# Two mixture-of-experts layers around an attention layer: the routing worked from the logits, and the slot-index matmuls moved to a place of their own

## The reference, cut to what matters

```python
x = x + 0.5 * ffn(layernorm(x)); x = x + attn(layernorm(x)); x = x + 0.5 * ffn(layernorm(x))   # x: 2 x 1024 x 128
def ffn(hidden_states):                        # N = 2048 tokens, E = 32 experts, TOP_K = 8, CAPACITY = 128, F = 96
    logits = x @ gate_weight.T
    probs = softmax(logits); topw, topi = top_k(probs, 8); topw = topw / topw.sum(-1, keepdims=True)
    pos = (cumsum(one_hot(flat_e), axis=0) * one_hot).sum(-1) - 1      # place in the expert's queue
    buf = zeros(E, 128, 128).at[flat_e, pos].set(flat_x, mode='drop')  # only the first 128 tokens of an expert
    gate, up = split(einsum('ech,efh->ecf', buf, gate_up_proj))
    eo = einsum('ecf,ehf->ech', silu(gate) * up, down_proj)
    out = (eo.at[flat_e, pos].get(fill_value=0) * flat_w[:, None]).sum(over the 8)
```

## Time and profile before

| what | before |
|---|---|
| time, median of 3 runs | 618.35 us (617.75 to 620.77) |
| the profiled execution: its own time, its span | 620.18 us, 618.5 us |
| granted clock of TensorE over the span | 0.928 |
| busy: PE, DVE, ACT, POOL | 529.7 us (86%), 431.8 (70%), 253.3 (41%), 94.9 (15%) |
| the chain that ended last | PE 69%, DVE 18%, issue 5%, ACT 4%, DMA 2% |
| DMA | 32.47 MB, mean 52 GB/s |

### The profile page before, as it was taken

How to read it: one execution, slowest core, us unless ns; L and a number is a source line. 1 busy time by engine, 2 the same in 40 slices (tenths; PEclk the granted TensorE clock), 3 DMA queues, 4 the chain that set the end, 5 groups by cost and what they waited for, 6 DMA issues and landing times.

```text
span 618.5 us, 11436 instructions
## 1 busy us (share of the span) xinstructions
PE 529.7 (86%) x3411; PEld 336.7 (54%) x3435; DVE 431.8 (70%) x1404; ACT 253.3 (41%) x405; POOL 94.9 (15%) x208
## 2 busy tenths in 40 slices
PE   2867999867798999999999999999987636899986
PEld 1745787653373555555555555555533533577764
DVE  5875888764659476777867677767810787879874
ACT  3523122123361456564555556554576320121212
POOL 3700000001500112131221212121222150000000
PEclk9679899987798799999999999999999758899999
DMA  8694221000061000000000000000020000112102
GB/s 232 176 283 138 76 77 45 32 2 3 0 258 67 1 21 26 12 25 27 27 27 26 28 16 25 15 26 27 0 80 0 1 1 0 39 47 71 49 27 69
DMA packets 27502, 32.47 MB, mean 52 GB/s; under 512 B 7009, under 2 KB 18753, under 8 KB 27329
## 3 DMA queue, kind: packets, MB, share of 16 engines
q1 hardware_dynamic: 26784, 31.61, 16.9%
q10 hardware_dynamic: 672, 0.28, 0.2%
HBM read 21.76 MB, written 9.96 MB: 51 GB/s over the span
## 4 chain that ended last, share of the span: by engine, by line
PE 69%; DVE 18%; issue 5%; ACT 4%; DMA 2%; SPq 1%; DVEq 1%; ACTq 0%; POOL 0%
PE ps L1271 12%; PE ps L1336 11%; PE ps L1061 10%; PE ps L1309 9%; PE ps L1093 7%; PE ps L1105 5%; DVE mxh L925 3%; PE ps L1112 3%; PE ps L1002 2%; DVE summed L922 2%; PE ps L1267 2%; ACT probs L663 1%; PE ps L1211 1%; PE ps L1065 1%; PE ps L1013 1%
## 5 line engine op out<-in xcount | busy, mean ns | idle before, releaser
L663 ACT ACTIVATE probs<-ps 128x1024 f32<-128x1024 f32 (+2 forms) x192 | 148.2, 810 | 128.1 <-PE ps L1309 128.0
L925 DVE TENSOR_REDUCE mxh<-ps 128x1 f32<-128x512 f32 (+2 forms) x176 | 117.5, 690 | 50.3 <-PE ps L1271 48.3
L1271 PE MATMUL ps<-Kst,Qst 120*128 120x512 f32 (+3 forms) x384 | 137.4, 422 | 7.5 <-DVE mxh L925 4.3
L1271 PEld LDWEIGHTS ps<-Kst,Qst 120*128 120x128 f32 x384 | 68.5, 196 | 66.8 <-DVE mxh L925 23.7
L1309 PE MATMUL ps<-Qst,Kst 121*128 121x512 f32 (+3 forms) x384 | 96.3, 357 | 1.9 <-ACT probs L663 1.7
L922 DVE CUSTOM_DVE_ANT_0 summed<-ps,maskf 128x384 f32<-128x384 f32 (+1 forms) x128 | 76.2, 621 | 23.1 <-PE ps L1271 21.3
L495 POOL TENSOR_SCALAR_AFFINE_SELECT probs<-probs 128x256 f32<-128x256 f32 x128 | 52.0, 406 | 232.5 <-ACT probs L663 231.8
L1336 PE MATMUL ps<-probs,Vst 128*32 128x512 f32 (+3 forms) x768 | 82.7, 503 | 1.2 <-POOL probs L495 1.2
L1309 PEld LDWEIGHTS ps<-Qst,Kst 121*128 121x128 f32 x384 | 67.5, 192 | 22.4 <-ACT probs L663 7.3
L1061 PE MATMUL ps<-onehot,xp 128*128 128x512 bf16 (+1 forms) x245 | 68.2, 397 | 9.5 <-DVE onehot L785 8.0
L785 DVE TENSOR_SCALAR onehot<-iotab,posm 128x128 bf16<-128x128 bf16 (+1 forms) x352 | 59.2, 247 | 3.3 <-issue 2.5
(11 more groups left out here) (167 smaller groups left out, 595.1 us busy)
## 6 DMA issues: line engine op xcount, KB each, us to landing
gus<-guT_d SPq DMA_DIRECT2D x14, 384.0 KB, 3.5
wgn<-in_L_ffn_gate_up_proj SPq DMA_DIRECT2D x8, 384.0 KB, 4.9
guT_d<-gus SPq DMA_DIRECT2D x8, 384.0 KB, 4.6
dns<-dnT_d SPq DMA_DIRECT2D x14, 192.0 KB, 3.4
Kst<-kn_d SPq DMA_DIRECT2D x28, 64.0 KB
Qst<-qn_d SPq DMA_DIRECT2D x28, 64.0 KB
wdn<-in_L_ffn_down_proj SPq DMA_DIRECT2D x8, 192.0 KB, 5.5
dnT_d<-dns SPq DMA_DIRECT2D x8, 192.0 KB, 5.1
```

The lines of the kernel that those rows point to most:

```text
L663: e.activation(probs[n % RING][:, 2 * b:2 * b + 2, lo:BANK], ps[:, 2 * b:2 * b + 2, lo:BANK], ACT.Exp, scale=SCALE).then_inc(probs_ready, 1)
L925: e.tensor_reduce(to, s.rearrange("p (q k) -> p q k", k=w), AX.X, ALU.max).then_inc(mx_ready, 1)
L1271: ins = e.matmul(ps[:, bank, i * w:(i + 1) * w], Qst[p][h][0:ROWS, column(b, jt * P):column(b, jt * P) + P], Kst[p][h][0:ROWS, column(b, o ...
```

## The change

- `route` reads the logits from a copy that ScalarE makes (`copy_logits`), takes the eight largest of them directly, and leaves the softmax and the weights out of the path to `posm`.
- The 15 position matmuls become one: VectorE first sums the mask over the tiles up to each tile, with four additions of shifted copies (`upto[1]` to `upto[4]`, shifts 1, 2, 4 and 8, over zeroed pads that GpSimd writes).
- The weights are made by `weigh`, on VectorE between the one-hots of chunks 0 and 1, and their three parts by GpSimd in `write_info`, after its `split`.
- The small index matmuls leave `gather` and become `find(c)`, run in step `c` after `gather(c + 1)`; the one-hots get a second buffer, and `slots(c)` runs in step `c` in the place where `slots(c + 1)` ran. ScalarE's `eoh` of `c` still waits for `slots(c)`.
- `exps(0)` follows the fourth weight copy on ScalarE instead of preceding the second.

```diff
-        maskb = sb("maskb", [P, NT, E], BF16, moe)
+        upto = [sb(f"upto{i}", [P, NT // 2 + NT, E], BF16, moe) for i in range(5)]
+        maskb = upto[0][:, NT // 2:, :]
...
-        onehot = sb("onehot", [P, NT, CE, CAP], BF16, moe)
+        onehot = [sb(f"onehot{p}", [P, NT, CE, CAP], BF16, moe) for p in range(RING)]
...
             def split(k):
+                for i in range(4):
+                    e.memset(upto[i][:, 0:NT // 2, :], 0.0).then_inc(pads, 1)
...
+            def write_info(k):
+                e.wait_ge(pr_ready, k + 1)
+                e.tensor_copy(info[:, :, :, 2], pr[:, :, :]).then_inc(info_step, 1)
+                e.wait_ge(info_step, 3 * k + 1)
+                e.tensor_tensor(wr[:, :, :], pr[:, :, :], info[:, :, :, 2], ALU.subtract).then_inc(info_step, 1)
+                e.wait_ge(info_step, 3 * k + 2)
+                e.tensor_copy(info[:, :, :, 3], wr[:, :, :]).then_inc(info_step, 1)
+                e.wait_ge(info_step, 3 * k + 3)
+                e.tensor_tensor(info[:, :, :, 4], wr[:, :, :], info[:, :, :, 3], ALU.subtract).then_inc(info_ready, 1)
             split(0)
+            write_info(0)
...
+            def copy_logits(k):
+                e.wait_ge(logits_done, k + 1)
+                e.activation(flat(wr[:, :, :]), ps[:, 2, :], ACT.Copy).then_inc(lg_copied, 1)
             def exps(k):
-                e.wait_ge(soft, 2 + 5 * k)
...
             copy_weights(0, 0)
-            exps(0)
+            copy_logits(0)
             copy_weights(1, 1)
-            with e.Fori(1, NCH // RING) as i:
-                for p in range(RING):
-                    e.wait_ge(w_stored[p], 32 * i)
-                    copy_weights(i * RING + p, p)
+            for s in range(RING, NCH):
+                e.wait_ge(w_stored[s % RING], 32 * (s // RING))
+                copy_weights(s, s % RING)
+                if s == RING + 1:
+                    exps(0)
             experts(0)
...
-                s0 = 5 * k
-                lg = ps[:, 2, :].rearrange("p (t e) -> p t e", t=NT)
...
-                e.wait_ge(logits_done, k + 1)
-                e.tensor_reduce(top[:, :], lg, AX.X, ALU.max).then_inc(soft, 1)
-                e.wait_ge(soft, s0 + 1)
-                e.tensor_tensor(zl[:, :, :], lg, wide_of(top), ALU.subtract).then_inc(soft, 1)
-                e.wait_ge(exp_done, k + 1)
-                e.tensor_reduce(den[:, :], zl[:, :, :], AX.X, ALU.add).then_inc(soft, 1)
-                e.wait_ge(soft, s0 + 3)
-                e.reciprocal(rden[:, :], den[:, :]).then_inc(soft, 1)
-                e.wait_ge(soft, s0 + 4)
-                e.tensor_tensor(pr[:, :, :], zl[:, :, :], wide_of(rden), ALU.mult).then_inc(soft, 1)
-                e.wait_ge(soft, s0 + 5)
+                e.wait_ge(lg_copied, k + 1)
                 for t in range(NT):
-                    e.max(t8[:, t, :], pr[:, t, :]).then_inc(top8, 1)
+                    e.max(t8[:, t, :], lg[:, t, :]).then_inc(top8, 1)
                 e.wait_ge(top8, NT * (k + 1))
                 for t in range(NT):
-                    e.match_replace(rep[:, t, :], t8[:, t, :], pr[:, t, :], -1.0).then_inc(replaced, 1)
+                    e.match_replace(rep[:, t, :], t8[:, t, :], lg[:, t, :], LOWEST).then_inc(replaced, 1)
                 e.wait_ge(replaced, NT * (k + 1))
-                q0 = 8 * k
-                e.tensor_scalar(maskb[:, :, :], rep[:, :, :], 0.0, None, ALU.is_lt).then_inc(routed, 1)
-                e.tensor_reduce(den[:, :], t8[:, :, :], AX.X, ALU.add).then_inc(routed, 1)
-                e.wait_ge(routed, q0 + 2)
-                e.reciprocal(rden[:, :], den[:, :]).then_inc(routed, 1)
-                e.tensor_tensor(wr[:, :, :], pr[:, :, :], maskb[:, :, :], ALU.mult).then_inc(routed, 1)
-                e.tensor_scalar(zl[:, :, :], rep[:, :, :], 0.0, UNROUTED, ALU.is_ge, ALU.mult).then_inc(posm_ready, 1)
-                e.wait_ge(routed, q0 + 4)
-                e.scalar_tensor_tensor(out=pr[:, :, :], in0=wr[:, :, :], scalar=0.25, in1=wide_of(rden), op0=ALU.mult, op1=ALU.mult).then_inc(routed, 1)
-                e.wait_ge(routed, q0 + 5)
-                e.wait_ge(info_const, 2 * (k + 1))
-                e.tensor_copy(info[:, :, :, 2], pr[:, :, :]).then_inc(routed, 1)
-                e.wait_ge(routed, q0 + 6)
-                e.tensor_tensor(wr[:, :, :], pr[:, :, :], info[:, :, :, 2], ALU.subtract).then_inc(routed, 1)
-                e.wait_ge(routed, q0 + 7)
-                e.tensor_copy(info[:, :, :, 3], wr[:, :, :]).then_inc(routed, 1)
-                e.wait_ge(routed, q0 + 8)
-                e.tensor_tensor(info[:, :, :, 4], wr[:, :, :], info[:, :, :, 3], ALU.subtract).then_inc(onehot_ready[k], 1)
+                e.tensor_scalar(maskb[:, :, :], rep[:, :, :], TAKEN, None, ALU.is_lt).then_inc(routed, 1)
+                e.wait_ge(routed, k + 1)
+                e.wait_ge(pads, 4 * (k + 1))
+                for i in range(4):
+                    src, half = upto[i], NT // 2
+                    e.tensor_tensor(upto[i + 1][:, half:, :], src[:, half:, :], src[:, half - (1 << i):half + NT - (1 << i), :], ALU.add).then_inc(summed_up, 1)
+                    if i < 3:
+                        e.wait_ge(summed_up, 4 * k + i + 1)
+                e.tensor_tensor(zl[:, :, :], lg[:, :, :], t8[:, :, 0:1].broadcast_to([P, NT, E]), ALU.subtract).then_inc(soft, 1)
+                e.tensor_scalar(rep[:, :, :], rep[:, :, :], TAKEN, UNROUTED, ALU.is_ge, ALU.mult).then_inc(posm_ready, 1)
...
+            def weigh(k):
+                e.wait_ge(exp_done, k + 1)
+                e.tensor_tensor(wr[:, :, :], zl[:, :, :], maskb[:, :, :], ALU.mult).then_inc(weigh_step, 1)
+                e.wait_ge(weigh_step, 3 * k + 1)
+                e.tensor_reduce(den[:, :], wr[:, :, :], AX.X, ALU.add).then_inc(weigh_step, 1)
+                e.wait_ge(weigh_step, 3 * k + 2)
+                e.reciprocal(rden[:, :], den[:, :]).then_inc(weigh_step, 1)
+                e.wait_ge(weigh_step, 3 * k + 3)
+                e.scalar_tensor_tensor(out=pr[:, :, :], in0=wr[:, :, :], scalar=0.25, in1=wide_of(rden), op0=ALU.mult, op1=ALU.mult).then_inc(pr_ready, 1)
...
-                    e.wait_ge(gathered, u + 1)
+                    e.wait_ge(indexed, u + 1)
...
                         place_slots(c - 1, 1 - p)
-                    if ahead >= 1:
-                        slots(c + 1, 1 - p)
+                    slots(c, p)
...
-                    if ahead >= 2:
-                        onehots(c + 2)
-                onehots(0)
-                slots(0, 0)
-                onehots(1)
+                    if ahead:
+                        onehots(c + 2, p)
+                onehots(0, 0)
+                weigh(k)
+                onehots(1, 1)
...
-                e.wait_ge(routed, 8 * k + 1)
-                e.matmul(ps[:, 3, :], zerosb[:, 0:P], zerosb[:, :], start=True, stop=False, skip_group_check=True)
-                for t in range(NT - 1):
-                    o = ps[:, 3, (t + 1) * E:].rearrange("p (t e) -> p t e", e=E)
-                    e.matmul(o, onesb[:, :], maskb[:, t:t + 1, :].broadcast_to([P, NT - 1 - t, E]),
-                             start=False, stop=False, skip_group_check=True)
-                e.matmul(ps[:, 3, :], beforeb[:, :], flat(maskb[:, :, :]), start=False, stop=True, skip_group_check=True).then_inc(pos_done, 1)
+                e.wait_ge(routed, k + 1)
+                e.matmul(ps[:, 3, :], beforeb[:, :], flat(maskb), start=True, stop=False, skip_group_check=True)
+                e.wait_ge(summed_up, 4 * (k + 1))
+                e.matmul(ps[:, 3, E:], onesb[:, :], flat(upto[4][:, NT // 2:NT // 2 + NT - 1, :]), start=False, stop=True,
+                         skip_group_check=True).then_inc(pos_done, 1)
...
                     u = k * NCH + c
                     e.wait_ge(bufT_ready, u + 1)
+                    def tile(t, first=False, last=False):
+                        e.wait_ge(onehot_ready[k], c * n + t + 1)
+                        for part in range(3):
+                            ins = e.matmul(ps[:, 0, :], xp[:, bass.ds(t, 1), part, :].rearrange("p o d -> p (o d)"),
+                                           onehot[p][:, bass.ds(t, 1), :, :].rearrange("p o e c -> p (o e c)"),
+                                           start=first and part == 0, stop=last and part == 2, skip_group_check=True)
+                        if last:
+                            ins.then_inc(gathered, 1)
...
+                def find(c, p):
...
                     e.wait_ge(idx_ready, u + 1)
+                    e.wait_ge(info_ready, k + 1)
...
-                            ins = e.matmul(ps[:, 3, q * 8:q * 8 + 5], onehot[:, bass.ds(t, 1), q, :].rearrange("p o c -> p (o c)"),
+                            ins = e.matmul(ps[:, 3, q * 8:q * 8 + 5], onehot[p][:, bass.ds(t, 1), q, :].rearrange("p o c -> p (o c)"),
```

(23 more changed lines are left out.)

30 lines of the change are left out of this document (14 added, 16 removed).

## The result

| | before | after |
|---|---|---|
| time, median | 618.68 us (617.75 to 620.77, 4 runs) | 641.99 us (634.62 to 648.47, 4 runs) |
| ratio | 1 | 1.0328, 95% interval 1.0288 to 1.0367 |
| the profiled execution, its span | 620.18, 618.5 | 634.62, 632.8 |

The change costs 3.3%, some 20 us. The ratio leaves out the run of 648.47 us, which was in a slower state that some executions show; the medians, which take it in, are 23 us apart. The prediction was 619.2, with a range up to 623.0: the time lies far above it, on the side of the third rival. The profiled execution is the fastest of the four, so the trace shows only 14.3 us of loss.

The account below looks back on a forecast made before the run. TensorE was taken to pace the middle steps, VectorE close behind; VectorE alone bounds the second routing. First layer -3.7 + 2.2 + 1.5 = 0.0, second -3.3 + 2.4 + 1.5 + 0.3 = +0.9: 619.2 us against 618.35, range 614.4 to 623.0.

Parts of the forecast that it names:

- the third rival: The series of index matmuls on TensorE isn't hidden: 628 us at the worst, 624 in the middle; chance 0.12.
- the last term of the steps: Index matmuls in one series on TensorE: the queue runs ahead under row matmuls, 0.3 us added in the second stage.
- The sign that the prediction had named: Gaps over 0.4 us in TensorE's index series would show the prediction wrong.
- late slots: Middle steps: `eoh` waits for `wslot`, now computed in the same step, so VectorE idles; +2.2 and +2.4 us per stage.
- Routing: Second layer's routing: one-hots start 6.6 us earlier, near 511.1, with four additions of 0.45 us each.
- The exclusion of GpSimd and the one-hots: Second start: GpSimd's 5.9 us and chunk 1's 4.0 us of one-hots run one after the other; gain 3.3, not 7.3.
- Rival (1): GpSimd and the one-hots don't exclude each other, so the second start keeps 7.3: 615.2 us; chance 0.17.
- First layer: First layer's start: the last weight transpose starts at 45.1, gate/up of chunk 0 at 48.2, a gain of 3.7 us.
- rival (2): The starts gain more as weight loads finish earlier, or `eoh` waits less: 2 to 4 us less, 616; chance 0.10.
- The last step: Last step of each layer: no one-hots hide the late slots, so `eol`, `place` and `combine` come later; +1.5 us.
- The queue of 64 entries: TensorE's queue, by the skill, would hold a whole series of 24 pairs, so the 0.3 us may be less.

Follow-up runs that it names:

- run 9: The changed kernel, but in the middle steps the index matmuls of chunk c stand between the row matmuls of chunk c + 1's gather: 620.89 us, ratio 1.0012.
- Kernel 1: The changed kernel with index matmuls back inside the gather from chunk 2 on and slots again a step ahead: 613.95 us, ratio 0.9908.
- 3: The changed kernel with the series reading a fixed column of `info` (output wrong): 621.82 us, ratio 1.0046.
- 5: The changed kernel, complete, with TensorE's loop over the chunks written out: 623.63 us, ratio 1.0091.
- 4: The changed kernel with the index series of chunk c ahead of the gather of chunk c + 1, from chunk 1 on: 642.98 us, ratio 1.0374.
- run 2: The kernel before, old routing, with only the index matmuls moved into their own series, two one-hot buffers and same-step slots: 644.18 us, ratio 1.0404.

## Why the prediction was wrong

The step that failed is the last term of the steps: "The first stage has 3.2 us of row matmuls to run ahead in; in the second, with one more turn of both loops, I add **0.3**." The sum put nothing for the series in the first stage and 0.3 in the second; with its longer steps it cost about 20 us. The reasoning took the lead for granted. The row matmuls give time to run ahead in, but the sequencer can't use the first half of it. Its operations come in the order of the list, and the gather's loop tile has a wait for that tile's one-hots in front of its matmuls. VectorE makes those one-hots while the gate/up and the row matmuls run. In the step at 66.73, kernel after:

```profile
66.50 3.33 DVE L798 TENSOR_SCALAR onehot<-iotab,posm 128x128 bf16<-128x128 bf16 x20
...
L1070 PEldq FUSED_REGOPS  x3: 46/46/89, 69.2 to 69.5; - x3
```

The first 16 one-hots, which the loop tile needs, are done near 69.2 (an estimate: 66.50 and 16/20 of 3.33), and there the sequencer goes on. It comes to the series at 70.2, half way through the gather, and the 12 operations up to 71.6 use up all that is left. In every middle step of both stages the first operation of the series comes 0.3 to 0.7 us behind the end of the one-hots. How long it comes before the series then goes with the series' length: in the second stage 2.7 us ahead in the two steps whose series take 1.9 and 2.0 us, 2.0 ahead with 2.7, and 1.3 to 1.4 ahead with 3.2 and 3.3. This is read from the trace of after; no run moved the one-hots. The sign that the prediction had named, gaps over 0.4 us in the index series, is in the longer ones: 0.16, 0.53 and 0.18 from 575.46 on.

The times, as ratios to the kernel before, divide the change in three (the ratio of 9 less that of 1, and so on; each difference is uncertain by 0.5 percentage points or so):

| part | predicted | measured |
|---|---|---|
| new routing, with the split weights (1) | -3.7 - 3.3 = -7.0 | -0.92%, -5.7 us |
| late slots, series of the first and last steps (9 less 1) | 2.2 + 2.4 + 1.5 + 1.5 = +7.6 | +1.04%, +6.4 us |
| the series of the middle steps (after less 9) | +0.3 | +3.16%, +19.6 us |

Kernel 1 keeps two short series at the start of a layer, so the first row is a lower bound of the gain by some tenths.

Point by point, in the trace of after:

- **Routing.** Right: 6.40 for 6.6, additions 0.45 each.
- **The exclusion of GpSimd and the one-hots.** Right in kind, too strict in size. The trace before had it only for `rem`; now 20 one-hots take 7.81 us beside GpSimd in the first layer (3.35 alone) and 24 take 8.40 (3.99). Rival (1) is out. The prediction let the two run one after the other, 5.9 + 4.0 = 9.9 us; 8.40 is 1.5 less, though GpSimd's four took 6.5 with their hand-offs and not 5.9. The gate/up matmuls of chunk 1 start at 531.29, 4.1 earlier (predicted 3.3). The Trainium skill (SBUF — State Buffer, section "Who interferes with whom") says that `tensor_scalar` can take the port pair that VectorE shares with GpSimd, and that the other then blocks for the whole instruction; the trace agrees that the one-hots contend, and the 8.40 us also show that not all of GpSimd's time is lost to VectorE.
- **First layer.** 46.45 instead of 48.2, because the last transposes began at 43.20 and not 45.1; the loads landed earlier in this execution, and later in others. In the median that is rival (2), neither won nor lost.
- **Late slots.** Right in mechanism, right in size in the first stage and twice too large in the second (run 9), but hidden in the kernel after: `eoh` waits there mostly for TensorE, whose down matmuls stand behind the series. Waits of the middle steps, first stage:

```profile
ACT eoh L591 <- PE ps L1139: 11.6, 5, 2.5
DVE eol L846 <- ACT eoh L591: 8.7, 5, 1.9
```

  Only with the series made cheap (3, 5, 9) does it show. So it doesn't add to the 19.6 of the series: taking the series away alone, or the late slots alone (4), gives different sums.
- **The last step.** Predicted +1.5. From the gate/up matmuls of chunk 7 to the end the second layer takes 21.5 us, against 20.1 before (632.8 - 611.27 and 618.5 - 598.44, the kernel before's from its timeline): +1.5. `place` of the chunk before and the slots stand ahead of `eoh` and `eol`, as worked out:

```profile
615.16 2.20 DVE L828 TENSOR_SCALAR place<-iota_s,tok 128x768 fp32r<-128x768 f32 x4
...
619.18 1.13 DVE L846 SCALAR_TENSOR_TENSOR eol<-ps,wslot,eoh 128x128 fp32r<-128x128 f32 x4 [1.26 <-ACT eoh L591]
...
621.24 0.62 PE L1119 MATMUL ps<-place,eoh 128*128 128x512 f32 x2 [0.42 <-DVE place L828]
```

- **Rival (3)** had the mechanism and, for the shortest steps, the size: 0.15 us per pair, steps of 10.5 and 11.4, and the rows say 10.62 and 11.37. That half would be hidden was a guess that came out. It had a chance of 0.12 and a worst case of 628. What it lacked is in the second stage: series longer than in the first, and the clock. The six steps grow by 17.0 us (611.27 - 531.29, against 598.44 - 535.42). Of these, 6 x 1.17 = 7.0 are what the step of 11.37 has over the old 10.20, and 4.0 are the longer series of four steps (3.32, 3.23, 2.70 and 2.67 us against 1.97). The other 6 are the lower clock: each of these four series is followed by a stretch at 0.50, as at 578.60, and these steps last 13.6 to 14.3 us with a mean clock of 0.87 to 0.88. The first step (12.80) has a lower clock too, at its start, but so had the first step of the kernel before (11.80).

The median of after is 7 us above the profiled execution. Its attention, which the change doesn't touch, ran 4.5 us faster than in the profile of before (364.0 us from ScalarE's first copy of the first layer's sums to that of the logits, against 368.5 to VectorE's first reading of them), with the granted clock at 0.91 from 160 to 200 us instead of 0.81. The profile thus understates the loss.

The queue of 64 entries that the prediction took from the Trainium skill (Advanced Engine Details and Errata, "Engine Queue Depths") was not what ran out at the series: in the steps shown here 12 to 16 of its pairs, 24 to 32 instructions, were waiting when it began. By the trace, the sequencer's wait for the one-hots and its own pace set the lead.

The run of the index matmuls alone (2) separates the clock from the series once: its step at 553.66 has a series of 3.25 us and stays at the full clock, 12.70 us long against 11.21 with a series of 1.78. So 1.5 us come with the longer series by itself, and the 14.20 and 14.32 of the kernel after have another 1.5 from the clock. What stays open is why a series of this length is followed by the lower clock in most steps and not in that one. Open too is how much would come back if the one-hots were ready a step earlier.

## What to carry to other kernels

Count the work of an engine's sequencer and not only the engine's: a matmul whose address contains a loop variable cost its queue some 0.13 us here, which is free under a row matmul of 0.2 us and sets the pace in a series of small ones; such instructions belong between long ones, or in code written out with constant addresses. When an argument rests on a queue that runs ahead, look in the trace for when its sequencer reaches the place, not for how much time it might have. Look there too for waits in the list ahead of that place: here a wait for one-hots cut the lead in half. And price a rival with what it sets off: in the second stage the gaps on TensorE came with a lower clock in four of six steps, which added 6 us to 11.

## What the runs showed of the hardware that was not expected

- A series of 20 pairs, a load of 128 x 128 weights and a matmul of five columns each, takes 0.51 us with fixed columns or the chunk loop written out, and 1.84 us with one register operation for each.
- Splitting the weights on GpSimd beside the one-hots takes as long as splitting them on VectorE ahead of the one-hots (8.40 against 7.9 us in the second layer), while a cast on ScalarE beside 16 one-hots costs them nothing (2.69 us).
- Behind a series of 3.23 us, in which TensorE was busy 2.31, the granted clock was 0.50 from 578.6 to 581.9; run 2 has a series of 3.25 us without it. The attention, the same in both kernels, took 4.5 us less in one profiled execution than in the other.
- The sequencer's lead over TensorE was 2.7 us in some steps and 1.3 in others of the same loop, and the series took 2.0 or 3.3 us accordingly.
